# The GRU stage of a two-layer graph kernel: wider inverse-transform products, one-pass distances, inputs last in each gate, and a GRU end of three operations

## The reference, cut to what matters

```python
h = conv1d(relu(bn(conv1d(xc, conv1_w, 0))), conv2_w, 8)      # 17 taps over the nodes
x_conv = relu(bn(h) + xc)
s = x @ w_se.T + b_se                                         # 3 values a node
dist = sq[:, :, None] + sq[:, None, :] - 2 * s @ s^T          # sq = sum(s * s)
A = exp(-dist) * mask                                        # the mask is adj
x_nmp = A @ relu(x @ w_msg.T + b_msg)
gi = concat(x_conv, x_nmp) @ w_ih.T + b_ih;  gh = x @ w_hh.T + b_hh
r = sigmoid(gi_r + gh_r);  z = sigmoid(gi_z + gh_z)
n = tanh(gi_n + r * gh_n)
out = layernorm(x + (1 - z) * n + z * x)
```

## Time and profile before

| what | value |
|---|---|
| median of three runs | 2299.92 us (2299.1 to 2303.17) |
| the profiled execution, its own time | 2302.35 us |
| its span | 2300.6 us |
| PE busy | 2064.0 us, 90% of the span |
| DVE, ACT, POOL busy | 1486.3, 1166.6, 665.7 us (65%, 51%, 29%) |
| chain that ended last | PE 51%, of it gates (L1377, `c_ps_g`) 35% |

### The profile page before, as it was taken

One profiled execution on the slowest core, in us unless ns is written; L12 is line 12 of the kernel. 1 busy time (PEld: TensorE's weight loads), 2 busy tenths in 40 slices (PEclk: granted clock), 3 DMA queues, 4 the chain that ended last, 5 costly groups with the idle time before them and its releaser, 6 DMA issues.

```text
span 2300.6 us, 38025 instructions
## 1 busy us (share of the span) xinstructions
PE 2064.0 (90%) x11782; PEld 1755.6 (76%) x11782; DVE 1486.3 (65%) x2773; ACT 1166.6 (51%) x2110; POOL 665.7 (29%) x563
## 2 busy tenths in 40 slices
PE   6888788888588878985899999999999999999998
PEld 5777667777488867774788888888888888888886
DVE  6798787988577766664555655556555655556554
ACT  6677666676355556663344444444444444444442
POOL 5676566676100000000122222222222222222222
PEclk9999999999799989998799999999999999999999
DMA  3554455544422257777121212212121212112100
GB/s 123 198 205 174 160 204 199 197 161 169 162 82 82 82 151 230 230 230 229 34 82 48 86 45 84 69 59 76 52 79 50 85 44 85 68 60 76 67 30 26
DMA packets 204611, 263.06 MB, mean 114 GB/s; under 512 B 12554, under 2 KB 158704, under 8 KB 203376
## 3 DMA queue, kind: packets, MB, share of 16 engines
q1 hardware_dynamic: 204528, 262.14, 34.2%
HBM read 174.01 MB, written 88.08 MB: 114 GB/s over the span
## 4 chain that ended last, share of the span: by engine, by line
PE 51%; issue 1%; ACT 1%; DMA 1%; DVE 0%; SPq 0%; POOL 0%; POOLq 0%; ACTq 0%; DVEq 0%
PE c_ps_g L1377 35%; PE c_ps_s L1404 5%; PE c_ps_m L1377 4%; PE c_ps_s L1377 2%; PE c_ps_s L1448 1%; PE c_ps_y L1427 1%; PE c_ps_y L1464 1%; PE c_ps_m L1464 1%; DMA c_yf<-y_spec 1%; PE c_ps_m L1465 0%; PE c_ps_y L1465 0%; ACT c_wi_h L1138 0%; SPq L1029 0%; DVE c_t L1246 0%; ACT c_yo L1125 0%
## 5 line engine op out<-in xcount | busy, mean ns | idle before, releaser
L1200 POOL TENSOR_TENSOR c_cl<-c_xc,c_ch 128x512 fp32r<-128x512 f32 x64 | 82.6, 1290 | 488.0 <-ACT c_ch L1092 470.6
L1276 DVE TENSOR_SCALAR c_work<-c_work 128x512 f32<-128x512 f32 x64 | 27.4, 428 | 219.3 <-ACT c_work L1087 219.3
L824 PE MATMUL m_ps<-m_wh,m_xl 128*128 128x256 f32 (+1 forms) x406 | 136.7, 337 | 34.4 <-issue 17.4
L1377 PE MATMUL c_ps_g<-c_xh,c_wh_l 128*128 128x512 f32 x384 | 155.6, 405 | 4.2 <-POOL c_cl L1200 4.2
L1377 PE MATMUL c_ps_g<-c_ch,c_wi_l 128*128 128x512 f32 x384 | 153.8, 401 | 0.0
L1377 PE MATMUL c_ps_g<-c_xl,c_wh_h 128*128 128x512 f32 x384 | 152.4, 397 | 0.0
L1377 PE MATMUL c_ps_g<-c_ch,c_wi_h 128*128 128x512 f32 x384 | 152.1, 396 | 0.0
L1377 PE MATMUL c_ps_g<-c_xh,c_wh_h 128*128 128x512 f32 x384 | 151.9, 396 | 0.0
L1377 PE MATMUL c_ps_g<-c_nh,c_wi_l 128*128 128x512 f32 x384 | 151.8, 395 | 0.0
L1377 PE MATMUL c_ps_g<-c_cl,c_wi_h 128*128 128x512 f32 x384 | 151.7, 395 | 0.0
L1377 PE MATMUL c_ps_g<-c_nh,c_wi_h 128*128 128x512 f32 x384 | 151.7, 395 | 0.0
(11 more groups left out here) (226 smaller groups left out, 7140.8 us busy)
## 6 DMA issues: line engine op xcount, KB each, us to landing
w_spec<-a_spec SPq DMA_DIRECT2D x8, 4352.0 KB, 16.8
m_w<-w_spec SPq DMA_DIRECT2D x68, 512.0 KB, 3.9
a_xt<-in_x_t SPq DMA_DIRECT2D x64, 256.0 KB, 2.9
a_xn<-in_x_n SPq DMA_DIRECT2D x64, 256.0 KB, 6.6
x_t<-a_x1t SPq DMA_DIRECT2D x64, 256.0 KB, 2.8
s_x<-x_t SPq DMA_DIRECT2D x64, 256.0 KB, 3.0
y_spec<-m_y SPq DMA_DIRECT2D x64, 256.0 KB, 2.4
c_x<-x_t SPq DMA_DIRECT2D x32, 512.0 KB, 3.8
```

Source lines behind the costliest of these rows:

```text
L824: last = nc.tensor.matmul(out.rearrange("p r (q c) -> p r q c", q=CHUNKS), xx[:, v, c, part], ww[:, v, c].rearrange("p q r c -> p r q c")[ ...
L1200: nc.gpsimd.tensor_tensor(cl[:, v, j], xc[:, j], ch[:, v, j].bitcast(F32), ALU.subtract).then_inc(s_cl, 1)
L1276: nc.vector.tensor_scalar(zz[:, :], tz[:, :], 0.5, 0.5, ALU.mult, ALU.add).then_inc(s_zz, 1)
L1377: last = nc.tensor.matmul(out, stationary, moving, start=(n == 0), stop=(n == len(passes) - 1))
```

## The change

- **Inverse transform.** `di` holds the high and the low part of the matrix side by side, and one product of `yh` with 256 columns makes both into two halves of a `ps_m` bank (`ps_inv`); `yl` with 128 columns follows. The remaining 8 spectrum rows of all four graphs are stacked as 96 rows, and one product of 256 columns (`dr`, zero outside a graph's own rows) serves two graphs. Half 0 moves ahead of gate Z 0 and half 1 behind gate IN 1; the result goes to `ps_m` and no longer to `ps_s`, so it waits until `mpre` has been read from there (`s_mpre`).
- **xconv.** ACT makes `xs` = `xg` + shift, as two operations, right behind `r_tanh` 0 and ahead of `sq`. DVE adds the two halves of `ps_inv` in two operations (`t2`), `ch` is the ReLU alone, and `cl` moves from GpSimd to DVE.
- **Distances.** ACT makes high parts of `left` and `right` and DVE a stack of 27 rows (`left_s`, `right_s`), and four fp32r products replace the fp32 ones.
- **Gates.** Own inputs first, then message sums, then convolution; the waits for `s_nl` and `s_cl` of gate R 0 stand ahead of the terms that need them.
- **GRU end.** yt = (tz + 3) x - (tz - 1) n in three DVE operations (twice the scale of before); x minus n and x plus n on GpSimd are gone, and the epsilon of the layernorm is scaled to match.
- **Orders.** ACT: output of go ahead of `mh`; `ch` 0 ahead of `z_tanh` 0; `n_tanh` 1 ahead of `ch` 1. `y_rest` is laid out by graph. The peeled tail of `pipeline` starts at `units - units % unroll`, which is `units` in each of its calls here.

```diff
 # SP, step(i)
-                    if isinstance(i, int) and i <= 2:
-                        sp.wait_ge(s_k, 3)
                     for row, part in enumerate((0, 1, 0)):
-                        sp.dma_start(yr[2 * REST * row:2 * REST * (row + 1), v].bitcast(F32), y_rest[part, :, bass.ts(g, B)]).then_inc(s_yr[v], 16)
+                        rows = slice(row * (RR // 3), (row + 1) * (RR // 3))
+                        sp.dma_start(yr[rows, v].bitcast(F32), y_rest[part, bass.ts(g, B)].rearrange("g d c -> (g d) c")).then_inc(s_yr[v], 16)
                 if live(2):
                     g = i - 2
-                    reached(sp, s_nx, 2 * g - 2)
+                    reached(sp, s_xa, 2 * g - 2)
                     sp.dma_start(xg[:, u], x1_t[:, :, bass.ts(g, T)]).then_inc(s_xg[u], 16)
 # ACT, step(i)
                     r_tanh(gg, 0)
                 if live(2):
+                    loaded(act, s_xg, 1, ga, v)
+                    reached(act, s_t2, 2 * KD * ga)
+                    for j in range(KD):
+                        nc.scalar.activation(xs[:, j], xg[:, v, j], ACT.Identity, bias=shift2[:, j:j + 1]).then_inc(s_xs, 1)
                     reached(act, s_s, ga + 1)
                     reached(act, s_d, ga)
                     nc.scalar.activation(sq[:, :], ps_s[0:NS, :], ACT.Square, bias=bs[:, 0:1]).then_inc(s_sact, 1)
...
+                    for side, (row, high) in enumerate(((left, left_h), (right, right_h))):
+                        reached(act, s_lr, 2 * ga + side + 1)
+                        nc.scalar.activation(high[:, :], row[:, :], ACT.Copy).then_inc(s_lrh, 1)
 # DVE
-            def xconv(g, u, j):
+            def xconv(g, j):
-                nc.vector.scalar_tensor_tensor(t2[:, j], ps_s[:, :], scale2[:, j:j + 1], xg[:, u, j], ALU.mult, ALU.add).then_inc(s_t2, 1)
-                nc.vector.tensor_scalar(xc[:, j], t2[:, j], shift2[:, j:j + 1], 0.0, ALU.add, ALU.max).then_inc(s_xc, 1)
+                nc.vector.scalar_tensor_tensor(t2[:, j].rearrange("p (b n) -> p b n", b=B), halves[:, 0], scale2[:, j:j + 1],
+                                               xs[:, j].rearrange("p (b n) -> p b n", b=B), ALU.mult, ALU.add).then_inc(s_t2, 1)
+                nc.vector.scalar_tensor_tensor(t2[:, j].rearrange("p (b n) -> p b n", b=B), halves[:, 1], scale2[:, j:j + 1],
+                                               t2[:, j].rearrange("p (b n) -> p b n", b=B), ALU.mult, ALU.add).then_inc(s_t2, 1)
+            def xconv_low(g, v, j):
+                nc.vector.scalar_tensor_tensor(cl[:, v, j], t2[:, j], 0.0, ch[:, v, j].bitcast(F32), ALU.max, ALU.subtract).then_inc(s_cl, 1)
-            def result(g, j):
+            def result(g, w, j):
+                nc.vector.scalar_tensor_tensor(xa, tz, 3.0, xg[:, w, j], ALU.add, ALU.mult).then_inc(s_xa, 1)
+                nc.vector.scalar_tensor_tensor(nb, tz, 1.0, nn, ALU.subtract, ALU.mult).then_inc(s_nb, 1)
+                nc.vector.tensor_tensor(yt[:, j], xa, nb, ALU.subtract).then_inc(s_yt, 1)
+                        nc.vector.scalar_tensor_tensor(stacked[:, :], high[:, :].bitcast(F32), mlow[:, side:side + 1], row[:, :],
+                                                       ALU.mult, ALU.add).then_inc(s_lrs, 1)
 # PE
-            def inverse(g, v, j):
-                for b in range(B):
-                    passes = ((yl[:, b, cols], di_h[:, 0]), (yh[:, b, cols], di_l[:, :]), (yr[:, v, b, cols], di_rest[:, :]),
-                              (yh[:, b, cols], di_h[:, 0]))
+            def inverse(v, j):
+                for h in range(2):
+                    for b in range(2 * h, 2 * h + 2):
+                        nc.tensor.matmul(ps_inv[:, b], yh[:, b, cols], di[:, :, :], start=(b % 2 == 0), stop=False)
+                        nc.tensor.matmul(ps_inv[:, b, 0], yl[:, b, cols], di[:, 0], start=False, stop=False)
+                    last = nc.tensor.matmul(ps_inv[:, 2 * h:2 * h + 2, 0], yr[:, v, cols],
+                                            dr[:, h * D:h * D + D].rearrange("p (b n) -> p b n", b=2), start=False, stop=True)
                 last.then_inc(s_inv, 1)
...
                     gate(IN_BANK[0], w, 2, 0, False, True).then_inc(s_gi, 1)
+                if live(2):
+                    reached(pe, s_yl, ga + 1)
+                    loaded(pe, s_yr, 3, ga, v)
+                    reached(pe, s_mpre, 2 * ga + 2)
+                    inverse(v, 0)
+                if live(3):
                     reached(pe, s_tr, 2 * g + 1)
                     gate(Z_BANK[0], w, 1, 0, True, True).then_inc(s_gz, 1)
                 if live(2):
-                    reached(pe, s_lr, 2 * ga + 2)
+                    reached(pe, s_lrs, 2 * ga + 2)
...
-                    inverse(ga, v, 0)
                     reached(pe, s_al, ga + 1)
                     reached(pe, s_ml, ga + 1)
+                    reached(pe, s_t2, 2 * (KD * ga + 1))
...
-                    inverse(ga, v, 1)
                 if live(3):
                     gate(IN_BANK[1], w, 2, 1, False, True).then_inc(s_gi, 1)
+                if live(2):
+                    reached(pe, s_ns, KD * ga + 1)
+                    inverse(v, 1)
```

More of the change, by code:

```diff
@@ L1331, in step @@
                                                    ALU.max, ALU.subtract).then_inc(s_ml, 1)
-                if live(3):
-                    result(gg, 0)
-                if live(2):
+                    for side, (row, high, stacked) in enumerate(((left, left_h, left_s), (right, right_h, right_s))):
+                        reached(dve, s_lrh, 2 * ga + side + 1)
+                        reached(dve, s_d, ga)
+                        nc.vector.scalar_tensor_tensor(stacked[:, :], high[:, :].bitcast(F32), mlow[:, side:side + 1], row[:, :],
+                                                       ALU.mult, ALU.add).then_inc(s_lrs, 1)
+                    xconv(ga, 0)
+                    xconv_low(ga, v, 0)
                     reached(dve, s_ea, ga + 1)
@@ L1378, in products, with gate @@
                 return last
-            def gate(bank, v, which, j, own, inputs):
+            def gate(bank, v, which, j, own, inputs, sums_of=None):
                 cols = slice(which * D + j * P, which * D + j * P + P)
+                out = ps_g[:, bank, :]
                 terms = []
                 if own:
-                    terms += [(wh_h[:, k, cols], wh_l[:, k, cols], xh[:, v, k], xl[:, v, k]) for k in range(KD)]
+                    terms.append(((lambda k: wh_h[:, k, cols]), (lambda k: wh_l[:, k, cols]), xh, xl, None))
@@ L1386, in gate @@
                 if inputs:
-                    terms += [(wi_h[:, k, cols], wi_l[:, k, cols], ch[:, v, k], cl[:, v, k]) for k in range(KD)]
-                    terms += [(wi_h[:, KD + k, cols], wi_l[:, KD + k, cols], nh[:, v, k], nl[:, v, k]) for k in range(KD)]
-                return products(ps_g[:, bank, :], terms)
-            def inverse(g, v, j):
-                cols = slice(j * P, j * P + P)
-                if j == 0:
-                    reached(pe, s_yl, g + 1)
-                    loaded(pe, s_yr, 3, g, v)
-                    reached(pe, s_ea, g + 1)
-                else:
-                    reached(pe, s_t2, KD * g + 1)
-                for b in range(B):
-                    passes = ((yl[:, b, cols], di_h[:, 0]), (yh[:, b, cols], di_l[:, :]), (yr[:, v, b, cols], di_rest[:, :]),
-                              (yh[:, b, cols], di_h[:, 0]))
-                    for n, (stationary, moving) in enumerate(passes):
-                        last = nc.tensor.matmul(ps_s[:, b * P:b * P + P], stationary, moving, start=(n == 0), stop=(n == len(passes) - 1))
+                    terms.append(((lambda k: wi_h[:, KD + k, cols]), (lambda k: wi_l[:, KD + k, cols]), nh, nl, (s_nl, 1)))
@@ new lines, in gate @@
+                    terms.append(((lambda k: wi_h[:, k, cols]), (lambda k: wi_l[:, k, cols]), ch, cl, (s_cl, KD)))
+                count, total = 0, 3 * KD * len(terms)
+                for w_high, w_low, high, low, made in terms:
+                    if made is not None and sums_of is not None:
+                        reached(pe, made[0], made[1] * (sums_of + 1))
+                    for k in range(KD):
+                        for stationary, moving in ((w_low(k), high[:, v, k]), (w_high(k), low[:, v, k]), (w_high(k), high[:, v, k])):
+                            last = nc.tensor.matmul(out, stationary, moving, start=(count == 0), stop=(count == total - 1))
+                            count += 1
@@ L1444, in step @@
                 if live(2):
-                    reached(pe, s_lr, 2 * ga + 2)
+                    reached(pe, s_lrs, 2 * ga + 2)
                     for b in range(B):
                         cols = slice(b * P, b * P + P)
-                        last = nc.tensor.matmul(ps_s[:, cols], left[:, cols], right[:, cols], start=True, stop=True)
+                        last = nc.tensor.matmul(ps_s[:, cols], left_s[:, cols], right_s[:, cols], start=True, stop=True)
```

(4 more changed lines are left out.)

199 lines of the change are left out of this document (100 added, 99 removed).

## The result

The changed kernel takes 2481.27 us (2478.38 to 2483.39, 4 runs) against 2299.51 us: ratio 1.0786, interval 1.0767 to 1.0805. It is slower by 182 us; the forecast was 2460, range 2385 to 2500. Its span is 2481.5 us.

The account below looks back on a forecast made before the run. The prediction took PE's instruction stream as the bound. From the profiled 2302.35 us, -60 + 162 + 2 + 55 = +159 gave 2461, 2459 on the median, stated as 2460 us; range 2385 to 2500.

Parts of the forecast that it names:

- PE saves by the change: On PE, cheaper distances (0.74 us) and inverse transform (1.20 us) save 1.94 us a step, 60 us over 31 steps.
- idle PE ahead of half 0: PE waits for mpre before the inverse transform of half 0: 5.6 us in 29 steps, 162 us.
- loss of clock: PE's clock falls after each idle stretch in the GRU stage: 1.9 us in 29 steps, 55 us.
- start: Step 2, the filling of the pipeline, has xg late as well, mostly hidden by splitting the weights: +2 us.
- The new wait: On ACT, xs ahead of sq waits for xg, landing about T = 12.8 to 13.0; mpre ends at 19.1.
- a short and a middle case: Bounds for the clock loss per stall: 1.6 us from the restart at 532.21, 2.5 from the GRU stage's start.
- Rival 1: The stall ahead of half 0 comes, but PE's clock stays at 2.4 GHz: 2404 us, chance 0.22.
- Rival 2: The load of xg is in time, no stall, PE's step 35.05 us: 2240 us, chance 0.07.
- Rival 3: A second stall on PE, at the message sums, 1 us a step: 2490 us, chance 0.10.
- Engine load: DVE near 26 of 35 us a step and ACT near 18.5; neither becomes the bound by its load.

Follow-up runs that it names:

- e1: The changed kernel with ACT making xs behind the high parts of left and right, no longer ahead of sq: 2243.92 us, ratio 0.9744.
- e9: e1 with the old distances, four fp32 products of 9 rows without high parts and stack: 2258.36 us, ratio 0.9819.
- e2: The changed kernel with xg loaded ahead of x1 on SP, ACT's order left alone: 2251.28 us, ratio 0.9768.
- e4: The kernel before with ACT waiting for the load of xg ahead of sq, without making xs: 2310.51 us, ratio 1.0026.
- e3: The changed kernel with gate Z 0's 18 products done once more, uselessly, ahead of PE's wait for mpre: 2412.93 us, ratio 1.0477.
- e8: e1 with the gates' old order of terms and both waits ahead of gate R 0: 2252.43 us, ratio 0.9784.
- e6: The changed kernel with xg loaded second on SP, behind x1 and ahead of at, yf and yr: 2352.89 us, ratio 1.0202.
- e5: The changed kernel with gate Z 0 moved ahead of the inverse transform of half 0 on PE: 2425.05 us, ratio 1.0531.

## Why the prediction was right, step by step

The forecast was right in direction and place, and near in size. Its sum was +159 us against the profiled run; the span grew by 2481.5 - 2300.6 = 180.9. The terms:

| term | forecast | measured | from |
|---|---|---|---|
| PE saves by the change | 31 x 1.94 = -60 | 31 x 1.79 = -55 | steps of 36.99 and 35.20 (e1) |
| idle PE ahead of half 0 | 29 x 5.6 = 162 | 155.6, 29 times | PE's waits |
| loss of clock | 29 x 1.9 = 55 | 29 x 2.67 = 77 | 43.24 - 35.20 - 5.37 |
| start | +2 | +3 | remainder: 180.9 + 55 - 155.6 - 77 |

The first two terms were put 5 and 6 us too high and cancel each other, which is luck; the 22 us that the sum lacks are the clock.

- **What PE saves.** The inverse transform was forecast at 2.32 and takes 2.31 (e1). The distances were forecast at 0.44 and take 0.67 (e1), so they save 0.51 instead of 0.74; e9 gives 0.49. I had taken the pace of 128-column products inside a stream (0.110) for a block of four, and left out what changing over to them and back costs. In e1's rows the first starts 0.09 after the gate's last product is over, and the four take 0.58 from there to the next gate. The two parts make 1.21 + 0.51 = 1.72 of the 1.79; the last 0.07 I have not assigned.
- **The new wait.** The landing was put at T = 13.0, the end of `mpre` at 19.1 and the idle time at 5.6; they came at 12.9, 19.0 and 5.4. 29 steps have it, as forecast, and steps 32 and 33 take 35.20. e1 and e2 remove it from two sides; e4 shows that the same 7.8 us wait on ACT costs 0.3% where PE does not ask for `mpre` early.
- **The loss of clock** is the mis-sized term: 2.67 instead of 1.9. e3, which takes only the idling away, gives 2.8. PE's two example steps show the spread. In the restart behind 1522.10:1527.40 the clock had fallen while PE idled and was back 3.5 us after the restart; in the step at 1310.00 it was 0.50 for 6.7 us with PE busy for 6.0 of them:

```profile
1303.80:1309.30 5.50, 0.32 (x2) 0.00 (x0) 2.03 (x5) 3.67 (x6) 0.00 (x0) 0.99 0.00 0
1309.30:1316.00 6.70, 6.00 (x19) 5.23 (x20) 5.25 (x8) 4.18 (x9) 0.00 (x0) 0.50 0.19 78
1522.10:1527.40 5.30, 0.00 (x0) 0.00 (x0) 2.64 (x6) 3.57 (x8) 0.00 (x0) 0.70 0.00 0
1527.50:1531.00 3.50, 3.50 (x13) 3.29 (x14) 2.33 (x3) 3.26 (x6) 0.00 (x0) 0.50 0.37 150
1531.00:1551.00 20.00, 20.00 (x101) 16.43 (x100) 12.64 (x19) 6.66 (x10) 0.00 (x0) 1.00 0.00 0
```

  The steps are 42.51 = 35.20 + 5.40 idle + 1.9, and 44.04 = 35.20 + 5.88 + 3.0: about half of 3.5 and of 6.0 us of work. I had taken a value between a short and a middle case (1.6 and 2.5); the long one was not among my bounds. The middle case was also misread. I took the start of the GRU stage, with 0.50 for 5.3 us after 4.22 us of idling, for a fall with a dense stream behind it, but the clock was at 0.50 there well before that idling:

```profile
1094.28:1100.00 5.72, 4.92 (x22) 4.66 (x22) 3.67 (x5) 3.13 (x4) 0.00 (x0) 0.50 0.00 0
1100.00:1109.48 9.48, 7.88 (x36) 7.50 (x35) 5.80 (x5) 4.44 (x5) 1.28 (x1) 0.50 0.01 2
```

  So that row shows how long a low clock took to come back, and none of the prediction's rows showed a fall in a stream as dense as this one. That 1.9 came as near to 2.67 as it did is in part luck. The rule of the Trainium skill (TensorE: Matmul & The Clock Gate, "HAM oscillation — how this bites in real kernels"), that a wait for a load in each round lets the clock fall in each round, is what this kernel shows: not one of the 28 measured steps is shorter than 41.97, where 40.6 would be the idle time alone.
- **The start** had 15.45 us of waiting for `mpre` on PE where the kernel before had 10.29 for the distances; e1 has 10.66. How the rest of the start makes up for these 5 us I have not followed. The +3 in the table is no measure of it: the first matmul of the GRU stage is at 1080.78 us where it was at 1078.02, so 2.8 of them lie ahead of the stage, inside the spread of the twelve profiles (e8 above).
- **Rivals.** Rival 1 (clock unharmed) falls with the two windows at 0.50 above, and e3 prices it: its 2404 is what the filler nearly reaches, 2413, by holding the clock. Rival 2 (the load is in time) was wrong of this kernel, and its price of 2240 is the measured 2244 of e1. Rival 3 (a second stall at the sums) did not come: PE's waits have no row for them.
- **Engine load.** DVE was put near 26 and ACT near 18.5 us; they need 25.2 and 17.5 in e1. Neither binds.

What stays open is what decides, at 2 to 3 us of idling, whether the clock falls in a step or not; e6 shows both outcomes, not in the order of the lengths, and I did not part them. How much of the gain of e1 comes from each of the remaining parts (the GRU end, cl on DVE) was not tried; since PE alone binds there, they can matter in the steady steps only through PE's waits, and it has none.

## What to carry to other kernels

When work is moved to an earlier place in an engine's fixed order, look up when its operand lands, and count everything that is queued behind it: here 1.3 us of work with a load that nobody had hurried cost 5.4 us of every step, and four lines decided between +7.9% and -2.5%. A late load is harmless as long as the engine that binds asks for nothing behind it; check a new edge from the same chain together with the move, for neither of the two cost much alone here (e4 has the wait without the edge, 0.3%; e2 has the edge with 0.7 us of the wait, and PE has no gap). An idle stretch on the saturated PE cost half as much again through the clock here (2.67 beside 5.37, 1.2 beside 2.4), so price both, and before filling it with real work ask who is late next.

## What the runs showed of the hardware

- The clock can fall behind quite short idle stretches in an otherwise dense stream, and their length alone does not decide it: in e6, 3.75 us of idling brought it to 0.50 for 3.4 us and 1.98 us to 0.51, while 2.08 and 3.06 us left it at 1.00; in e5, two stretches of at most 1.8 and 3.0 us a step cost some 1.8 us a step on top. In the changed kernel it fell in every step, and the two steps shown lost 1.9 and 3.0 us by it.
- Filling idle time with products that nobody reads can pay: e3 does 18 more products of 512 columns in each step and is 68 us faster than the changed kernel, since it holds the clock at 1.00.
- Four one-pass products of 128 columns between streams of 512 take 0.67 us and not 4 x 0.110 (e1); four fp32 ones took 1.18 (the kernel before).
